# Token differences and the third LayerNorm's normalisation on GpSimd, in a fused attention and channel-mixing kernel

## The chip, the cores and the metric

The kernel runs as one program on the 8 cores of one Trainium2 chip. Each core computes one half (2048 tokens) of one of four sequences, with 512 tokens ahead of it for the attention window. The metric is the device time in microseconds of the slowest core.

## The reference, cut to what matters

```python
x = x + _layernorm(_L0_attn_ref(_layernorm(x), w_qkv, w_out))      # 16 heads of 64, window 512, RoPE
x = x + _layernorm(_L0_ffn_ref(_layernorm(x), W_r, W_k, W_v, mu_r, mu_k))
...
# in _L0_ffn_ref
x_prev = jnp.concatenate([jnp.zeros((B, 1, C), x.dtype), x[:, :-1, :]], axis=1)
xr = mu_r * x + (1.0 - mu_r) * x_prev
xk = mu_k * x + (1.0 - mu_k) * x_prev
r = jax.nn.sigmoid(jnp.einsum('btc,dc->btd', xr, W_r))
k = jnp.einsum('btc,dc->btd', xk, W_k)
k_act = jnp.square(jax.nn.relu(k))
out = r * jnp.einsum('btc,dc->btd', k_act, W_v)
```

The model width is 1024. The kernel computes the two mixtures as `x_prev + mu * (x - x_prev)`, so each needs the token difference `x - x_prev` once.

## The kernel before, in words

Each core works through 20 tiles of 128 tokens. Tiles 0 to 2 give keys and values only; tiles 3 to 19 are also queries. The order of the work is written out by hand: `slot_table` places every step (`"k0"`, `"norm1"`, `"mix"`, ...) in a numbered slot, and each engine runs one program that loops over the slots and issues what it has in each, after waiting on semaphores. Slots are not times. An engine that has nothing to wait for runs ahead, and one that waits holds all that it has in later slots.

**Attention part.** A tile takes 16 slots, one per head. Per head TensorE makes scores (L583), VectorE adds the mask and takes the maximum (`row_max`, L764), ScalarE takes the exponential (`exps`, L935), a DMA transposes it, and TensorE weights the values (L604). Between the heads lie the next tile's projections (L520), the rotary embedding (VectorE L742 and L745, then an addition on GpSimd, L1096), the output projection (L674), and the second LayerNorm with its residual addition on GpSimd (L1106), which gives x2, the input of the second half. x2 is stored to a spill tensor in HBM.

**Second half.** Its 16 tiles are taken in four groups of four (`sup` 0 to 3); one more tile, i = 0, gives the token ahead. Per tile: `stats3` (VectorE statistics, L774 to L777), `rstd3` (ScalarE, L917 and L919), `norm3` (VectorE L787, `(x - mean) * rstd` from f32 to bf16), `tx` (TensorE transposes, L690), and `x2T_out` (ScalarE, into `x2T`, L950). When a group's tiles are in `x2T`, `mix_chunk` makes the inputs of its products in 8 chunks of 512 tokens, all on VectorE: the difference into `dch`, which is `xl2a` (L813), a drain, xk (L815) and xr (L817), the last two `scalar_tensor_tensor` with both tensor inputs in SBUF. From the second group on the first chunk also copies the last token of the group before (L805). The last chunk lets TensorE start on the group.

A group's products are 24 units of 8 matmuls each, one per slot, in the order of `UNITS`: eight `fk` (L703), then `fr` (L715) and `fv` (L730) mixed. ScalarE makes relu and square of `fk` (L956, L960) and the sigmoid of `fr` in three steps (L971, L973, L975). VectorE multiplies the sigmoid with `fv` and takes statistics (`ff_out`, L832 to L838); ScalarE applies the fourth LayerNorm (L1066), and GpSimd adds the residual (`ob`, L1124). Unit n of group `sup` is in slot `F_OFF + 24 sup + n`. The chunks of the next group's mixing lie in that group's slots 14 to 21, and its `tx` in slots 4, 6, 8 and 10. The first four tiles of `sup` 0 and tile i = 0 are handled early, during attention (`EARLY_SLOT`), and the mixing of `sup` 0 lies in slots 315 to 322, among the heads of the last attention tile.

Of the kernel before, what the change touches and what calls it, by code (L numbers as in the profile page):

```python
# [74 lines left out]
F_OFF = 329  # L75
# [15 lines left out]
CAST0 = 79  # L91
# [142 lines left out]
def build_nc():  # L234
# [27 lines left out]
    with es:  # L262
# [10 lines left out]
        with ExitStack() as p1:  # L273
# [505 lines left out]
            def norm3(ve, i):  # L779
# [5 lines left out]
                elif i >= 5:  # L785
                    ve.wait_ge(S["mm"], mm_no("qt", NT - 1))
# [457 lines left out]
```

## Time and profile before

| what | value |
|---|---|
| runs shown | median 730.37 us, 729.66 to 730.95, 3 runs |
| profiled execution | 729.59 us; span of the slowest core 728.1 us |
| spans of the eight cores | 723.4 to 728.1 us |
| busy in the span | TensorE 616.1, VectorE 560.3, ScalarE 537.6, GpSimd 207.5 us |
| granted TensorE clock, mean of the core shown | 0.965 |

The span runs from the first to the last instruction of the slowest core, and 1.5 us of the profiled time lie around it. Busy time is the time in which an engine executes something; where it waits for another engine the trace names the one that released it. Times in the rows are counted from the span's start.

### The profile page before, as it was taken

What the parts mean: (1) busy time and instruction counts of PE and PEld (TensorE: products, weight loads), DVE (VectorE), ACT (ScalarE), POOL (GpSimd) and SP (SyncE); (2) the same over time, 40 slices, a digit from 0 to 9 for tenths busy, and PEclk for the clock granted to TensorE, in tenths of its full rate; (3) what the DMA queues carried; (4) which work ended last, traced back from release to release, by engine and by line L of the source; (5) the groups of instructions that cost most, each with busy time, mean ns of one, the idle gap of its engine ahead of it and who ended that gap; (6) DMA issues with size and microseconds to landing.
All of it is one profiled execution on the core that took longest, in us unless ns stands there. A gap on an engine that the chain in (4) does not pass through costs nothing.

```text
span 728.1 us, 15852 instructions; the slowest of 8 cores (723.4 to 728.1 us)
## 1 busy us (share of the span) xinstructions
PE 616.1 (85%) x4680; PEld 326.2 (45%) x4680; DVE 560.3 (77%) x1143; ACT 537.6 (74%) x1060; POOL 207.5 (28%) x184
## 2 busy tenths in 40 slices
PE   1978799989989999989899999955997896896993
PEld 0434445545555545555555555523543442442441
DVE  3563788998998988989888988899559759759234
ACT  2135779888988988998888898856884784693773
POOL 3561032143143144134134313401013403303213
PEclk9999999999999999999999999985999999999998
DMA  7999889978998999989998876898824244313304
GB/s 171 180 185 156 146 152 178 174 148 163 168 152 153 164 156 183 172 157 181 154 164 162 151 159 133 157 249 190 234 94 187 67 145 145 112 63 116 116 1 173
DMA packets 202738, 111.21 MB, mean 153 GB/s; under 512 B 181408, under 2 KB 184736, under 8 KB 202272
## 3 DMA queue, kind: packets, MB, share of 16 engines
q1 hardware_dynamic: 197536, 95.52, 61.7%
q0 software_dynamic: 5120, 14.68, 13.5%
q8 instruction: 40, 0.66, 0.4%
q14 instruction: 42, 0.34, 0.2%
HBM read 62.99 MB, written 23.59 MB: 119 GB/s over the span
## 4 chain that ended last, share of the span: by engine, by line
PE 50%; DVE 18%; DVEq 10%; issue 10%; ACT 5%; POOL 2%; DMA 2%; ACTq 1%; SPq 0%; POOLq 0%
PE PS L520 19%; PE PS L583 6%; PE PS L674 6%; PE PS L715 5%; PE PS L703 4%; DVEq L834 4%; PE PS L604 3%; DVE sneg L764 3%; PE PS L513 3%; PE PS L533 3%; DVE tmpAB L745 2%; DVE tmpAB L742 2%; DVEq L814 2%; ACT Pn L935 2%; POOL kqnat L1096 2%
## 5 line engine op out<-in xcount | busy, mean ns | idle before, releaser
L764 DVE CUSTOM_DVE_ANT_0 sneg<-PS,mqs 128x640 f32<-128x640 f32 (+1 forms) x272 | 215.8, 813 | 51.5 <-PE PS L583 43.5
L935 ACT ACTIVATE Pn<-sneg,nm 128x640 bf16<-128x640 f32 (+1 forms) x272 | 221.2, 814 | 37.7 <-DVE nm L764 36.1
L520 PE MATMUL PS<-wbig,xll 128*128 128x512 bf16 x768 | 181.0, 379 | 6.4 <-DVE tmpAB L745 4.1
L583 PE MATMUL PS<-kT,qEO 128*128 128x128 bf16 (+3 forms) x656 | 113.5, 279 | 23.1 <-DVE nm L764 22.9
L1096 POOL TENSOR_TENSOR kqnat<-tmpAB 128x512 bf16<-128x512 f32 x74 | 94.4, 1278 | 114.0 <-DVE tmpAB L745 114.0
L520 PEld LDWEIGHTS PS<-wbig,xll 128*128 128x128 bf16 x768 | 69.4, 97 | 82.9 <-issue 11.8
L583 PEld LDWEIGHTS PS<-kT,qEO 128*128 128x128 bf16 x656 | 53.9, 98 | 65.6 <-issue 36.1
L1101 POOL TENSOR_SCALAR st<-st 128x1 f32<-128x1 f32 x17 | 4.5, 266 | 246.2 <-ACT st L919 246.2
L674 PE MATMUL PS<-wout_b,oTs 128*128 128x512 bf16 x272 | 64.2, 378 | 1.6 <-DVE sneg L832 1.0
L604 PE MATMUL PS<-v_nat,PT 128*128 128x64 bf16 x1344 | 62.4, 194 | 3.6 <-DMA PT<-Pn 2.5
L917 ACT ACTIVATE st<-st,sb_consts 128x1 f32<-128x1 f32 x70 | 20.4, 291 | 56.4 <-DVE st L890 22.8
L742 DVE TENSOR_TENSOR tmpAB<-PS,sb_tabs 128x512 f32<-128x512 f32 x74 | 50.8, 687 | 13.4 <-PE PS L533 9.3
L604 PEld LDWEIGHTS PS<-v_nat,PT 128*128 128x128 bf16 x1344 | 53.2, 99 | 16.1 <-issue 5.3
L730 PE MATMUL PS<-wbig,xll 128*128 128x512 bf16 x256 | 57.4, 379 | 0.0
L832 DVE TENSOR_TENSOR sneg<-PS,qEO 128x512 f32<-128x512 f32 x32 | 21.9, 684 | 44.2 <-PE PS L730 42.2
L935 ACT ACTIVATION_READ_ACCUMULATOR Pn<-sneg,nm 128x1 f32 x272 | 51.7, 190 | 0.0
L745 DVE TENSOR_TENSOR tmpAB<-PS,sb_tabs 128x512 f32<-128x512 f32 x74 | 50.4, 680 | 0.0
L1106 POOL TENSOR_TENSOR xb<-xb,t 128x1024 f32<-128x1024 f32 x17 | 40.3, 2370 | 12.2 <-ACT t L1048 12.2
L703 PE MATMUL PS<-Pn,wbig 128*128 128x512 bf16 x128 | 31.8, 412 | 10.7 <-DVE PT L817 10.7
L730 PEld LDWEIGHTS PS<-wbig,xll 128*128 128x128 bf16 x256 | 25.0, 98 | 30.3 <-issue 0.6
L513 PE MATMUL PS<-sb_ident,kqnat 128*128 128x128 bf16 x296 | 22.9, 221 | 18.2 <-POOL kqnat L1096 16.2
L674 PEld LDWEIGHTS PS<-wout_b,oTs 128*128 128x128 bf16 x272 | 24.3, 97 | 30.1 <-issue 4.6
(92 smaller groups left out, 932.6 us busy)
## 6 DMA issues: line engine op xcount, KB each, us to landing
xb<-x_ext SPq DMA_DIRECT2D x20, 512.0 KB, 4.9
x2spill<-xb SPq DMA_DIRECT2D x17, 512.0 KB, 3.0
wbig<-wqkv POOLq DMA_DIRECT2D x12, 512.0 KB, 21.4
wbig<-wff SPq DMA_DIRECT2D x12, 512.0 KB, 5.2
kT<-x2spill SPq DMA_DIRECT2D x9, 512.0 KB, 5.5
out<-kT SPq DMA_DIRECT2D x9, 512.0 KB, 3.0
tmpAB<-x2spill SPq DMA_DIRECT2D x8, 512.0 KB, 5.6
v_nat<-x2spill SPq DMA_DIRECT2D x7, 512.0 KB, 5.5
```

Source lines behind the costliest of these rows:

```text
L513: last = pe.transpose(PSb[:, col + c * 128:col + (c + 1) * 128], src[:, base + c * 128:base + (c + 1) * 128], ident[:])
L520: last = pe.matmul(PSf[:, col:col + 512], xlt_part(t, c * 128, 128), wslice(base, c, lo, 512), start=(c == 0), stop=(c == 7))
L583: last = pe.matmul(PSf[:, col:col + nb * 128], qq[:, qc:qc + 128], kT[:, kc:kc + nb * 128], start=True, stop=True)
L604: last = pe.matmul(PSf[:, col:col + 64], PT[:, pc:pc + 128], v_nat[:, vc:vc + 64], start=(kb == first_kb), stop=(kb == 4))
L674: last = pe.matmul(PSf[:, col:col + 512], oTs[:, c * 128:(c + 1) * 128], wout_b[:, c * 1024 + h * 512:c * 1024 + h * 512 + 512], start=(c ...
L703: last = pe.matmul(PSf[:, col:col + 512], wslice(1, c, j * 128, 128), xk_half[sup % 2][:, c * 512:c * 512 + 512], start=(c == 0), stop=(c ...
L730: last = pe.matmul(PSf[:, col:col + 512], kaT[:, c * 512 + o * 128:c * 512 + o * 128 + 128], wslice(2, c, h * 512, 512), start=(c == 0), s ...
L742: ve.tensor_tensor(bass.AP(tmpAB, toff, [[2048, 128], [64, 8], [32, 2], [1, 32]]), bass.AP(PS, base, [[4096, 128], [64, 8], [32, 2], [1, 3 ...
L745: ve.tensor_tensor(bass.AP(tmpAB, 1024 + toff, [[2048, 128], [64, 8], [32, 2], [1, 32]]), bass.AP(PS, base + 32, [[4096, 128], [64, 8], [- ...
L764: ve.tensor_tensor_reduce(out=sneg[:, dst + lo:dst + 640], in0=PSf[:, col + lo:col + 640], in1=mqs[:, mcol + lo:mcol + 640], scale=-0.125, ...
L935: sc.activation(Pn[:, dst + lo:dst + 640], sneg[:, src + lo:src + 640], AF.Exp, bias=nm[:, hc:hc + 1], scale=-1.0, accum_out=rs[:, hc:hc + ...
L1096: gp.tensor_tensor(dst[:, (i % 2) * 512:(i % 2) * 512 + 512], tmpA[:, toff:toff + 512], tmpB[:, toff:toff + 512], ALU.add).then_inc(S["nat ...
```

## The change

GpSimd takes two things from VectorE. `norm3` moves to the GpSimd program, for all 17 tiles. The difference becomes a step of its own, `"dif"`, on GpSimd: `difference` writes it to the place where xr will stand (`xr_half`), and VectorE's chunk then makes xk from it and xr in place, after a wait on the new semaphore `dif`. The drain between the difference and the two others is gone, and the copy of the last token moves along. For `sup` 0 the eight differences are spread over slots 192 to 297, for the others they stand four slots ahead of their chunks. Other slots are set anew: the second half starts one slot earlier (`F_OFF` 329 to 328), `norm3` two slots earlier in its group, `ob`, `store` and `res` one or two later, the loads of the `fr` weights two later, and the slots of the first tiles and the bank rotation's end (`HEAD_END`) change. Branches for tiles 90 and up never apply, as there are 20 tiles.

```diff
-    3: {"xload": -22, "tabload": -22, "stats1": -8, "rstd1": -5, "norm1": 1, "x": 3,
-        "k0": 31, "k1": 32, "kt": 40, "qt": 44, "v0": 67, "v1": 68},
+    3: {"xload": -23, "tabload": -22, "stats1": -6, "rstd1": -5, "norm1": 2, "x": 5,
+        "k0": 31, "k1": 33, "kt": 40, "qt": 42, "v0": 67, "v1": 68},
...
-KG = 28
-QG = 37
-V0_SLOT = {"0": 59, "1": 60, "2": 62, "3": 64}
+KG = 26
+QG = 35
+V0_SLOT = {"0": 59, "1": 60, "2": 61, "3": 62}
...
-F_OFF = 329
+F_OFF = 328
...
-EARLY_SLOT = {"stats3": 54, "rstd3": 56, "norm3": 58, "tx": 60}
-MASK_OFF = 0
+EARLY_SLOT = {"stats3": 54, "rstd3": 56, "norm3": 59, "tx": 60}
+MASK_OFF = -1
...
-ITEM_SLOT = {"ld": -6, "stats3": -1, "rstd3": -1, "norm3": 1, "tx": 3}
+ITEM_SLOT = {"ld": -6, "stats3": -1, "rstd3": -1, "norm3": -1, "tx": 3}
...
-OUT_LAG = {"ff": 2, "rstd4": 2, "nb4": 2, "t2": 3, "ob": 3, "store": 7, "res": 0}
-WF_SLOT = {"wfk": 303, "wfr": 310, "wfv": 321}
+
+DIF0 = 192
+DIF_STEP = 15
+DIF_LEAD = 4
+OUT_LAG = {"ff": 2, "rstd4": 2, "nb4": 2, "t2": 3, "ob": 4, "store": 9, "res": 1}
+WF_SLOT = {"wfk": 303, "wfr": 312, "wfv": 321}
...
-HEAD_END = 59
+HEAD_END = 49
...
+            table[("dif", F_OFF + 24 * sup - MIX_LEAD + c - DIF_LEAD)] = 8 * sup + c
+        table[("dif", DIF0 + DIF_STEP * c)] = c
...
-                d = dch[:, (c % 2) * 512:(c % 2) * 512 + 512]
-                x = bass.AP(x2T, cur + c * 520 + 8, [[8320, 128], [1, 512]])
-                xp = bass.AP(x2T, cur + c * 520 + 7, [[8320, 128], [1, 512]])
-                ve.tensor_tensor(d, x, xp, ALU.subtract)
-                ve.drain()
-                ve.scalar_tensor_tensor(xk_half[sup % 2][:, c * 512:(c + 1) * 512], d, mus[:, 8 + c:9 + c], xp,
-                                        ALU.mult, ALU.add)
-                last = ve.scalar_tensor_tensor(xr_half[sup % 2][:, c * 512:(c + 1) * 512], d, mus[:, c:c + 1], xp,
-                                               ALU.mult, ALU.add)
+                d = xr_half[sup % 2][:, c * 512:(c + 1) * 512]
+                xp = bass.AP(x2T, cur + c * 520 + 7, [[8320, 128], [1, 512]])
+                ve.wait_ge(S["dif"], u + 1)
+                ve.scalar_tensor_tensor(xk_half[sup % 2][:, c * 512:(c + 1) * 512], d, mus[:, 8 + c:9 + c], xp,
+                                        ALU.mult, ALU.add)
+                last = ve.scalar_tensor_tensor(d, d, mus[:, c:c + 1], xp, ALU.mult, ALU.add)
...
+            def difference(gp, u):
+
+                sup, c = divmod(u, 8)
+                cur = (sup % 2) * 4160
+                if c == 0:
+                    gp.wait_ge(empty_sem("tx", 4 + 4 * sup), empty_cnt("tx", 4 + 4 * sup))
+                    if sup == 1:
+                        gp.wait_ge(S["av"], NQ * 8)
                     if sup >= 1:
                         prv = ((sup - 1) % 2) * 4160
-                        ve.tensor_copy(bass.AP(x2T, cur + 7, [[8320, 128], [520, 8], [1, 1]]),
+                        gp.tensor_copy(bass.AP(x2T, cur + 7, [[8320, 128], [520, 8], [1, 1]]),
                                        bass.AP(x2T, prv + 519, [[8320, 128], [520, 8], [1, 1]]))
-                        ve.drain()
+                        gp.drain()
                     if sup >= 2:
-                        ve.wait_ge(S["mm"], mm_no("fr", (sup - 2) * 8 + 7))
+                        gp.wait_ge(S["mm"], mm_no("fr", (sup - 2) * 8 + 7))
+                gp.tensor_tensor(xr_half[sup % 2][:, c * 512:(c + 1) * 512],
+                                 bass.AP(x2T, cur + c * 520 + 8, [[8320, 128], [1, 512]]),
+                                 bass.AP(x2T, cur + c * 520 + 7, [[8320, 128], [1, 512]]),
+                                 ALU.subtract).then_inc(S["dif"], 1)
...
+                if i >= 2:
+                    ve.wait_ge(S["xl2"], i - 1)
...
+            def norm3(gp, i):
+                gp.wait_ge(S["rstd3"], i + 1)
+                if 1 <= i < 5:
+                    gp.wait_ge(S["mm"], mm_no("tx", i - 1))
+                elif i >= 7:
+                    gp.wait_ge(S["mm"], mm_no("tx", i - 2))
+                elif i >= 5:
+                    gp.wait_ge(S["mm"], mm_no("qt", NT - 1))
+                gp.tensor_scalar(xl2_part(i, 0, 1024), x2_tile(i), stat2(st3, i, 12, 1),
+                                 stat2(st3, i, 14, 1), ALU.subtract, ALU.mult).then_inc(S["xl2"], 1)
```

## Rows read from the trace of the kernel before

**Rows 1.** The page: the span and the busy times of the engines.

```profile
span 728.1 us, 15852 instructions; the slowest of 8 cores (723.4 to 728.1 us)
...
PE 616.1 (85%) x4680; PEld 326.2 (45%) x4680; DVE 560.3 (77%) x1143; ACT 537.6 (74%) x1060; POOL 207.5 (28%) x184
```

**Rows 2.** Waits of the whole span: who waited for whom, us in total, times, longest.

```profile
PE PS L583 <- DVE nm L764: 22.9, 25, 3.3
...
PE PS L703 <- DVE PT L817: 10.7, 2, 6.6
...
PE PS L703 <- DVE xr L817: 6.9, 1, 6.9
...
PE PS L690 <- DVE kqnat L787: 4.2, 4, 1.9
```

**Rows 3.** Windows: busy time of each engine by stretch, clock, DMA share, GB/s.

```profile
102.00:204.00 102.00, 93.23 (x861) 53.05 (x856) 92.96 (x208) 90.24 (x188) 30.59 (x30) 1.00 0.91 162
...
480.00:500.00 20.00, 6.88 (x66) 4.13 (x63) 19.34 (x36) 8.29 (x18) 2.86 (x2) 0.64 0.95 222
...
506.40:564.60 58.20, 53.19 (x334) 26.06 (x332) 40.99 (x68) 41.27 (x77) 8.45 (x6) 1.00 0.57 183
564.60:619.40 54.80, 45.16 (x224) 20.69 (x224) 40.93 (x64) 37.15 (x67) 14.16 (x10) 0.94 0.35 120
619.40:672.70 53.30, 45.15 (x225) 20.68 (x226) 39.80 (x62) 35.41 (x64) 11.38 (x8) 0.95 0.26 90
672.70:716.30 43.60, 43.60 (x192) 19.09 (x192) 14.32 (x25) 30.81 (x54) 10.13 (x8) 0.95 0.26 92
```

**Rows 4.** Timeline of VectorE, the mixing among the last heads: start, us, what.

```profile
475.91 0.42 DVE L813 TENSOR_TENSOR xl2a<-x2T 128x512 bf16<-128x512 bf16 x1
...
477.75 0.82 DVE L764 CUSTOM_DVE_ANT_0 sneg<-PS,mqs 128x640 f32<-128x640 f32 x1
...
500.06 0.81 DVE L764 CUSTOM_DVE_ANT_0 sneg<-PS,mqs 128x640 f32<-128x640 f32 x1
```

**Rows 5.** Timeline of TensorE: the start of groups 1, 2 and 3, idle time in brackets.

```profile
564.59 8.53 PE L703 MATMUL PS<-Pn,wbig 128*128 128x512 bf16 x32 [4.06 <-DVE PT L817]
...
619.43 8.42 PE L703 MATMUL PS<-xb,wbig 128*128 128x512 bf16 x32 [6.91 <-DVE xr L817]
...
672.66 16.01 PE L703 MATMUL PS<-Pn,wbig 128*128 128x512 bf16 x64 [6.64 <-DVE PT L817]
```

**Rows 6.** Groups of instructions by line and shape: busy us, mean ns of one.

```profile
L1096 POOL TENSOR_TENSOR kqnat<-tmpAB 128x512 bf16<-128x512 f32 x74 | 94.4, 1278 | 114.0 <-DVE tmpAB L745 114.0
...
L835 DVE BATCH_NORM_STATS2 st<-sneg 128x6 f32<-128x512 f32 x32 | 22.2, 694 | 3.3 <-issue 0.4
L832 DVE TENSOR_TENSOR sneg<-PS,qEO 128x512 f32<-128x512 f32 x32 | 21.9, 684 | 44.2 <-PE PS L730 42.2 <-POOL kT L1124 1.9
L1124 POOL TENSOR_TENSOR kT<-kT,sneg 128x1024 f32<-128x1024 f32 x9 | 21.1, 2348 | 18.1 <-ACT sneg L1066 18.1
...
L815 DVE SCALAR_TENSOR_TENSOR xb<-xl2a,sb_mus,x2T 128x512 bf16<-128x512 bf16 x16 | 15.9, 992 | 1.2
L813 DVE TENSOR_TENSOR xl2a<-x2T 128x512 bf16<-128x512 bf16 x32 | 14.9, 464 | 0.4
...
L1116 POOL TENSOR_SCALAR st<-st 128x1 f32<-128x1 f32 x15 | 6.6, 440 | 101.0 <-ACT st L919 101.0
...
L787 DVE TENSOR_SCALAR xl2a<-xb,st 128x1024 bf16<-128x1024 f32 x5 | 4.0, 808 | 0.0
```

**Rows 7.** Timeline of all engines in group 1: GpSimd beside VectorE's two-input instructions.

```profile
593.88 1.01 ACT L950 ACTIVATE x2T<-PS 128x1024 bf16<-128x1024 bf16 x1
...
601.75 0.39 POOL L1116 TENSOR_SCALAR st<-st 128x1 f32<-128x1 f32 x1 [18.61 <-ACT st L919]
...
603.69 2.37 POOL L1124 TENSOR_TENSOR v_nat<-v_nat,sneg 128x1024 f32<-128x1024 f32 x1 [1.54 <-ACT sneg L1066]
603.77 2.84 DVE L817 SCALAR_TENSOR_TENSOR xr<-xl2a,sb_mus,x2T 128x512 bf16<-128x512 bf16 x1
...
613.23 0.77 POOL L1116 TENSOR_SCALAR st<-st 128x1 f32<-128x1 f32 x1 [7.17 <-ACT st L919]
```

More of the change, by code:

```diff
@@ L86 @@
 MIX_LEAD = 10
-OUT_LAG = {"ff": 2, "rstd4": 2, "nb4": 2, "t2": 3, "ob": 3, "store": 7, "res": 0}
-WF_SLOT = {"wfk": 303, "wfr": 310, "wfv": 321}
+DIF0 = 192
[3 more added lines that the diff above has]
+WF_SLOT = {"wfk": 303, "wfr": 312, "wfv": 321}
 WF_STEP = 6
-CAST0 = 79
+CAST0 = 78
 CAST_STEP = 8
@@ L777, in stats3 @@
                 ve.bn_aggr(stat2(st3, i, 12, 2), stat2(st3, i, 0, 12)).then_inc(S["mv3"], 1)
-            def norm3(ve, i):
-                ve.wait_ge(S["rstd3"], i + 1)
-                if 1 <= i < 5:
-                    ve.wait_ge(S["mm"], mm_no("tx", i - 1))
-                elif i >= 7:
-                    ve.wait_ge(S["mm"], mm_no("tx", i - 2))
-                elif i >= 5:
-                    ve.wait_ge(S["mm"], mm_no("qt", NT - 1))
-                ve.tensor_scalar(xl2_part(i, 0, 1024), x2_tile(i), stat2(st3, i, 12, 1),
-                                 stat2(st3, i, 14, 1), ALU.subtract, ALU.mult).then_inc(S["xl2"], 1)
             def mix_chunk(ve, u):
@@ L802, in mix_chunk @@
                             ve.wait_ge(ptsem(pr), 16 * (pr // PR + 1))
+                    if sup >= 2:
+                        ve.wait_ge(S["mm"], mm_no("fr", (sup - 2) * 8 + 7))
+                d = xr_half[sup % 2][:, c * 512:(c + 1) * 512]
[3 more added lines that the diff above has]
+                                        ALU.mult, ALU.add)
@@ L803, in mix_chunk @@
+                last = ve.scalar_tensor_tensor(d, d, mus[:, c:c + 1], xp, ALU.mult, ALU.add)
+                if c == 7:
+                    last.then_inc(S["mix"], 1)
+            def difference(gp, u):
[5 more added lines that the diff above has]
+                        gp.wait_ge(S["av"], NQ * 8)
                     if sup >= 1:
@@ L819, in mix_chunk @@
-                if c == 7:
-                    last.then_inc(S["mix"], 1)
+                        gp.wait_ge(S["mm"], mm_no("fr", (sup - 2) * 8 + 7))
[3 more added lines that the diff above has]
+                                 ALU.subtract).then_inc(S["dif"], 1)
             def ff_out(ve, u):
@@ L868, in vector_program @@
                     if t is not None:
+                        if t >= 92:
+                            ve.wait_ge(S["xln"], t - 1)
                         ve.wait_ge(xsem(t), 16 * (t // XR + 1))
@@ L874, in vector_program @@
                     t = tile_at(n, "norm1")
-                    if t is not None:
+                    if t is not None and t < 90:
                         ve.wait_ge(S["rstd1"], t + 1)
@@ L890, in vector_program @@
                         ve.bn_aggr(stat(st2, t, 12, 2), stat(st2, t, 0, 12)).then_inc(S["mv2"], 1)
-                    i = tile_at(n, "norm3")
-                    if i is not None:
-                        norm3(ve, i)
                     i = tile_at(n, "stats3")
@@ L1102, in gpsimd_program @@
                                          ALU.mult, ALU.mult).then_inc(S["nb2"], 1)
+                    t = tile_at(n, "norm1")
+                    if t is not None and t >= 90:
+                        gp.wait_ge(S["rstd1"], t + 1)
+                        gp.wait_ge(S["mm"], mm_no("x", t - 2))
+                        gp.tensor_scalar(xln[:, (t % 2) * 1024:(t % 2) * 1024 + 1024], x_tile(t), stat(st1, t, 12, 1),
+                                         stat(st1, t, 14, 1), ALU.subtract, ALU.mult).then_inc(S["xln"], 1)
+                    i = tile_at(n, "norm3")
+                    if i is not None:
+                        norm3(gp, i)
+                    u = tile_at(n, "dif")
+                    if u is not None:
+                        difference(gp, u)
                     t = tile_at(n, "add2")
```

7 lines of the change are left out of this document (3 added, 4 removed), and 12 rows, old and new, of tables (HEAD_SLOT, SEMS).

## The prediction

> **What bounds the kernel now.** I read the page first, for the busy times: TensorE leads with 616.1 of 728.1 us, VectorE follows with 560.3, and GpSimd has the room, 28% [rows 1]. An average says little here, so I cut the span into stretches [rows 3]. The reader is to see three regimes. In the attention part (one stretch of 102 us shown) TensorE has 93.2, VectorE 93.0 and ScalarE 90.2 us of 102: three engines hold each other, none is alone the bound. From 480 to 500 us VectorE has 19.3 us of 20 and TensorE 6.9: there VectorE alone is the bound, and the granted clock falls to 0.64. In the second half groups 0, 1 and 2 take 58.2, 54.8 and 53.3 us, while group 3, which has no mixing behind it, takes 43.6 with TensorE busy throughout. So what groups 1 and 2 have over about 43.5 us is waiting.
>
> The waits say for whom [rows 2]: TensorE waited 22.9 us for `row_max`, most of it between 478 and 504 us, 17.6 us for the last xr of a mixing (three times), and 4.2 us for norm3. The timelines place them. The mixing of group 0 runs from 475.91 to 500.06, eight chunks with seven heads' maxima and the one at 500.06 behind them [rows 4]. At the start of groups 1, 2 and 3 TensorE stood idle for 4.06, 6.91 and 6.64 us, and then ran its first four units in 8.5 us where later ones take 6.9 (at 1.2 instead of 2.4 GHz for some of it) [rows 5].
>
> **What the change takes from VectorE.** The difference takes 0.42 us, and with the drain a chunk goes from 1.84 us (475.91 to 477.75) to the two remaining instructions, 1.84 - 0.50 = 1.34 us [rows 4]. The mean of 464 ns over 32 holds a few that were held up [rows 6]. norm3 takes 0.81 us of VectorE per tile where nothing holds it [rows 6].
>
> **What it adds to GpSimd.** No row shows a bf16 difference or a wide `tensor_scalar` on GpSimd. The floor is the one-column instruction of L1116, mean 0.44 us; the ceiling is the two-input addition of 1024 f32, 2.35 us; the nearest row is the two-input addition of 512 elements with bf16 output, 1.28 us, and I take that for the difference [rows 6]. For norm3 (1024 elements, one tensor input) I take 1.3 us, between the same ends. Nothing hangs on it: in the second half norm3 stands ready four slots before its transposes, and GpSimd is busy for 14.2 of 54.8 us in group 1 [rows 3]. With the new work that becomes about 14.2 + 8 x 1.28 + 4 x 1.3 = 29.6 us. If that cover were gone, TensorE's 4.2 us of waits for norm3 would stay. The new wait in `stats3` only keeps a statistics slot from being overwritten two tiles on; behind it in VectorE's queue stands `ff_out`, and norm3 two tiles back is long done.
>
> **The cost that is not in the instruction times.** VectorE's two remaining mixing instructions read two SBUF tensors, and so does GpSimd's difference. The trace shows what happens when such a pair meets. At 603.69 GpSimd starts its residual addition and needs its usual 2.37 us; the xr instruction at 603.77 takes 2.84 us instead of 0.75, and ends 0.55 us after GpSimd does [rows 7]. That is waiting, not sharing. It works the other way too: L1116 takes 0.39 us at 601.75 and 0.77 at 613.23, each time ending just behind a two-input VectorE instruction [rows 7]. The mean of 992 ns on L815 [rows 6] against 0.75 unheld is such collisions. The Trainium skill has a rule for it (SBUF — State Buffer, Who interferes with whom): a VectorE instruction with two SBUF inputs and a GpSimd instruction that reads SBUF exclude each other, the second waiting for the whole of the first. The trace agrees, with 2.84 against 0.75 us. By that rule the moved differences are not parallel to the mixing at all; without it each mixing would lose the full 4.0 us worked out below.
>
> **The sum, in the order of time.**
>
> Head (0 to 80 us): the order of TensorE's products there is nearly the same, and the first 20 us wait for loads. I take 0, with 1.5 us to either side.
>
> Attention: five norm3 leave VectorE, 5 x 0.73 us of queue time = 3.7 us. ScalarE and TensorE are as full as VectorE [rows 3], so I count a quarter: -0.9. The eight differences of group 0, 10 us in all, lie in slots that hold no rotary addition on GpSimd, and VectorE's heads read PSUM there; bounds 0 and -3.7.
>
> Mixing of group 0: here VectorE is the bound, and no difference runs beside it since all eight were made long before. 8 x 0.50 = 4.0 us come off in full: -4.0. The second half starts one slot earlier, in a stretch in which TensorE idles anyway: a head's spacing, about 1.6 us: -1.6.
>
> Mixings of groups 1, 2 and 3. I follow the one beside group 1. Its first `ff_out` starts at 593.8, and the last xr ends at 619.1, where TensorE had been free since 612.5 (619.43 - 6.91) [rows 5]. GpSimd's first difference must wait for `x2T_out` of the group's last tile, which ends at 593.88 + 1.01 = 594.9 [rows 7]. From then on 8 differences x 1.28 = 10.2 us and 16 instructions x 0.67 = 10.7 us exclude each other, so the end can't come before 594.9 + 20.9 = 615.8. If VectorE keeps its pairs together and its `ff_out` (0.68 + 0.69 us, one SBUF input or none [rows 6]) falls beside differences, I get 616.2: -2.9. If GpSimd gets in between every two VectorE instructions while it has differences queued, and its residual addition (2.35 us) gets in too, the differences run ahead and the mixing ends at about 620.5: +1.4. The 601.75 row (in between xk and xr) speaks for the second, the 613.23 row (past one more instruction) for the first. I take the middle, -0.8, for the mixings beside groups 1 and 2. For the one beside group 0 the same two countings give 561 and 564.8 against 564.1 before, because there the first difference can start two slots ahead of the first chunk: -1.2. Sum of the three: -2.8.
>
> Group 3 and the tail hold no mixing and no norm3: 0. `ob`, `store` and `res` later by a slot or two are waited for by nothing until the very end, where each is driven by its data.
>
> Total: -0.9 - 4.0 - 1.6 - 2.8 = -9.3 us against the execution's own 729.59, so 720.3. The median of the runs shown is 0.8 above that execution: 721.
>
> **The rivals.** What can be told from no change is about 0.2%, 1.5 us.
>
> *Forecast* (716 to 727), chance 0.48.
>
> *The exclusion costs little and TensorE becomes the bound* (chance 0.22). GpSimd's differences might slip into VectorE's `ff_out` times, or cost well under 1.28 us with bf16 inputs. Then the idle times before groups 1 to 3 and the waits for norm3 go, 17.6 + 4.2 = 21.8 us. Taking 70% of it, since ScalarE with 37.2 of 54.8 us [rows 3] runs some 5 us behind by `x2T_out`: 729.6 - 5.6 - 0.9 - 15.3 = 707.8, or 708 to 709 beside the median, 700 to 715 as ends. For it: the room on GpSimd. Against it: 594.9 as the first possible start.
>
> *Full alternation* (chance 0.18): each of the three mixings ends 1 to 1.5 us later than before, and only group 0's gain remains: 729.6 - 5.6 + 3.5 + 0.8 = 728, 727 to 731. Half of it counts as no change.
>
> *The difference is dear* (chance 0.12), the side on which it is slower. If the bf16 difference costs 2.35 us like the widest row [rows 6], each of the 24 differences of the later mixings adds 1.07 us to the excluded time: 24 x 1.07 = 25.7, so 720.3 + 25.7 = 746. It decides from 1.28 + 9.3/24 = 1.67 us on. For it: no row shows bf16 inputs on GpSimd, one of them at an odd element. Against it: 1.28 and 2.35 us are in proportion to the elements, not to bytes, since one writes bf16 and the other f32. The Trainium skill (GPSIMD Engine Reference, Engine selection) says that elementwise work belongs on VectorE, GpSimd being about twice slower with two inputs. The trace has 1.28 against 0.42 us, three times, and the rule is about the engine, not about which of them is waited for.
>
> **How the numbers follow.** Faster by over 0.2%: 0.48 + 0.22 + 0.08 = 0.78; within: 0.10; slower: 0.12. The range leaves out the dear difference, the deepest part of the TensorE case and the upper end of the alternation: 706 to 730; the forecast's own is 716 to 727.
>
> **What would show it.** L815 and L817 mean times above 1 us in the later mixings and near 0.75 in group 0's; the GpSimd difference near 1.28 us; 24 of the differences beside or between VectorE's pairs; the mixing of group 0 in about 20 us instead of 24; TensorE still idle for 3 to 8 us before groups 1 to 3; groups 1 and 2 at 52 to 56 us. Wrong it would be if those groups fall below 49 us, if the bf16 difference is far from 1.28 us, or if the attention part changes by more than 4 us.

## The result and the profile after

The changed kernel takes 734.27 us (median of 11 runs) beside 730.95 us of the kernel before (11 runs). The ratio is 1.0049, with a 95% interval of 1.0032 to 1.0066: slower by about 0.5%, or 3.6 us. Three of the 11 runs of before (754, 774 and 781 us) were in a slower state of the chip, and such runs are left out of all ratios here and of the means over runs, not of the medians. The forecast was 721 us, with a range of 706 to 730. It had the wrong sign.

The page of after, with its busy times, stands beside [rows 1]. The profiled execution took 738.41 us, which is the highest of the 11 runs, and the core shown is its slowest.

```profile
span 736.9 us, 15874 instructions; the slowest of 8 cores (724.8 to 736.9 us)
...
PE 624.0 (85%) x4680; PEld 327.4 (44%) x4680; DVE 536.4 (73%) x1091; ACT 538.9 (73%) x1060; POOL 311.8 (42%) x236
```

VectorE lost 24 us of work and GpSimd gained 104 us. By the forecast's prices, 32 differences of 1.28 us and 17 `norm3` of 1.3 us, GpSimd would have gained 63 us.

Because single cores lie up to 12 us apart, I compare stages by their mean over the eight cores of the profiled execution. The marks are the first row maximum (L764 before, L769 after: the end of the head) and the first `fk` product (L703, L708: the start of the second half). These are one execution of each kernel. Over all its runs the mean span of a kernel spreads by 0.2 to 1.0 us (standard deviation), and the execution shown of the changed kernel lies 1.5 us above the mean of its 11 runs (729.9 against 728.4), so differences below about 1 us say little.

| mean of 8 cores, us | head | attention to first fk | second half | span |
|---|---|---|---|---|
| before | 62.2 | 441.6 | 221.8 | 725.6 |
| after | 66.2 | 438.3 | 225.4 | 729.9 |
| difference | +4.0 | -3.3 | +3.6 | +4.3 |
| forecast | 0 | -6.5 | -2.8 | -9.3 |

The middle stage went the right way. The head and the second half went the wrong way, by 4.0 and 6.4 us against the forecast. The waits of the whole span say for whom in the second half; they answer to [rows 2].

```profile
PE PS L588 <- DVE nm L769: 28.0, 37, 2.9
...
PE PS L695 <- POOL kqnat L1089: 13.5, 7, 2.4
DVE st L781 <- POOL kqnat L1089: 10.5, 5, 4.8
...
PE PS L735 <- DVE sneg L840: 5.8, 4, 2.5
...
PE PS L538 <- DMA wbig<-wqkv: 5.2, 2, 3.7
...
PE PS L708 <- DVE PT L806: 3.2, 1, 3.2
...
PE PS L708 <- DVE xr L806: 2.6, 1, 2.6
```

TensorE's wait for the last xr before a group of products went from 17.6 us in three times to 5.8 in two, a larger fall than the forecast's. In its place stand 13.5 us in which it waits for `norm3` (L1089, now on GpSimd), where it was 4.2 us, and 7.1 us (5.8 at L735 and 1.3 at L708) in which it waits for `ff_out` (L840) to empty the PSUM bank that the next product needs, where it was 1.0. VectorE itself waits 10.5 us for `norm3` inside `stats3`. Another 5.2 us are waits of the query products (L538) for their weights' loads. The windows of after, beside [rows 3], show whose engine filled up (102 to 204 us of attention, 20 us around group 0's mixing, then groups 0, 1, 2 and 3):

```profile
102.00:204.00 102.00, 93.51 (x844) 52.53 (x845) 91.83 (x208) 89.78 (x185) 41.40 (x33) 1.00 0.99 156
...
484.00:504.00 20.00, 8.31 (x86) 5.19 (x84) 19.78 (x36) 10.77 (x24) 2.87 (x2) 0.72 1.08 219
...
509.30:567.90 58.60, 54.02 (x337) 26.25 (x335) 35.77 (x54) 41.28 (x77) 32.97 (x18) 0.99 0.57 170
567.90:624.50 56.60, 45.93 (x226) 20.80 (x226) 33.61 (x52) 37.77 (x68) 39.95 (x24) 0.97 0.37 121
624.50:681.50 57.00, 45.84 (x224) 20.71 (x224) 33.89 (x49) 35.76 (x64) 37.30 (x21) 0.96 0.28 84
681.50:725.30 43.80, 43.76 (x190) 19.21 (x191) 14.40 (x25) 30.86 (x54) 11.65 (x9) 0.93 0.27 97
```

In group 1 GpSimd is busy for 39.95 of 56.6 us, where the forecast had 29.6. Groups 1 and 2 take 56.6 and 57.0 us, not 52 to 56. Group 3, which holds no mixing and no norm3, takes 43.8 us, where it took 43.6. The prices are in the groups by form:

```profile
L1089 POOL TENSOR_SCALAR kqnat<-tmpAB,st 128x1024 bf16<-128x1024 f32 x8 | 30.2, 3778 | 12.5 <-PE PS L708 11.4 <-ACT st L926 1.2
...
L825 POOL TENSOR_TENSOR PT<-x2T 128x512 bf16<-128x512 bf16 x16 | 21.1, 1343 | 3.7 <-issue 3.7
...
L806 DVE SCALAR_TENSOR_TENSOR PT<-PT,sb_mus,x2T 128x512 bf16<-128x512 bf16 x16 | 19.5, 1216 | 0.0
...
L804 DVE SCALAR_TENSOR_TENSOR Pn<-PT,sb_mus,x2T 128x512 bf16<-128x512 bf16 x16 | 17.1, 1069 | 4.1 <-POOL PT L825 4.1
```

The difference (L825) costs 1.34 us in the mean, collisions with VectorE included, close to the 1.28 taken. `norm3` costs 3.78 us against 0.81 on VectorE [rows 6], where 1.3 was taken. The timeline of GpSimd in the first half of group 1 shows what that makes:

```profile
574.67 3.77 POOL L1089 TENSOR_SCALAR kqnat<-tmpAB,st 128x1024 bf16<-128x1024 f32 x1 [0.42 <-ACT st L926]
578.42 0.26 POOL L1146 TENSOR_SCALAR st<-st 128x1 f32<-128x1 f32 x1
578.65 2.36 POOL L1154 TENSOR_TENSOR kT<-kT,sneg 128x1024 f32<-128x1024 f32 x1
580.99 3.78 POOL L1089 TENSOR_SCALAR kqnat<-xb,st 128x1024 bf16<-128x1024 f32 x1
584.73 2.35 POOL L1154 TENSOR_TENSOR v_nat<-v_nat,sneg 128x1024 f32<-128x1024 f32 x1
587.07 3.77 POOL L1089 TENSOR_SCALAR kqnat<-tmpAB,st 128x1024 bf16<-128x1024 f32 x1
590.80 2.34 POOL L1136 TENSOR_TENSOR xb<-xb,t 128x1024 f32<-128x1024 f32 x1
593.13 3.78 POOL L1089 TENSOR_SCALAR kqnat<-tmpAB,st 128x1024 bf16<-128x1024 f32 x1
```

Look at the brackets: after the first line there are none, so GpSimd works without a pause from 574.67 to 596.9 us. Four `norm3` alternate with three residual additions, and each waits in the queue for the one ahead. TensorE's transposes stand right behind three of them, and stop the products of the group:

```profile
578.59 0.61 PE L695 MATMUL PS<-sb_ident,kqnat 128*128 128x128 bf16 x8 [2.16 <-POOL kqnat L1089]
...
584.91 0.85 PE L695 MATMUL PS<-sb_ident,kqnat 128*128 128x128 bf16 x8 [2.26 <-POOL kqnat L1089]
...
597.05 0.61 PE L695 MATMUL PS<-sb_ident,kqnat 128*128 128x128 bf16 x8 [2.01 <-POOL kqnat L1089]
```

### The profile page after: what moved, and what is told of

Its sections match the earlier page's. It is cut to its first block, busy times and chain, and to the rows that moved or that the text cites. A ratio compares the mean times of both kernels' runs of the same rounds, so it can differ in the third digit from the quotient of the medians.

```text
span 736.9 us, 15874 instructions; the slowest of 8 cores (724.8 to 736.9 us)
## 1 busy us (share of the span) xinstructions
PE 624.0 (85%) x4680; PEld 327.4 (44%) x4680; DVE 536.4 (73%) x1091; ACT 538.9 (73%) x1060; POOL 311.8 (42%) x236
## 4 chain that ended last, share of the span: by engine, by line
PE 44%; DVE 15%; issue 10%; DMA 10%; POOL 7%; ACT 5%; DVEq 5%; ACTq 2%; SPq 1%; POOLq 0%
PE PS L525 18%; PE PS L588 5%; DMA PT<-Pn 5%; PE PS L708 5%; PE PS L679 4%; PE PS L720 4%; DMA wbig<-wqkv 4%; POOL kqnat L1089 3%; DVEq L842 3%; PE PS L609 3%; DVE sneg L769 3%; PE PS L518 2%; ACT Pn L942 2%; DVE tmpAB L747 2%; PE PS L735 2%
## 5 line engine op out<-in xcount | busy, mean ns | idle before, releaser
L769 DVE CUSTOM_DVE_ANT_0 sneg<-PS,mqs 128x640 f32<-128x640 f32 (+1 forms) x272 | 216.4, 814 | 57.2 <-PE PS L588 53.3
L525 PE MATMUL PS<-wbig,xll 128*128 128x512 bf16 x768 | 184.8, 385 | 5.9 <-DVE tmpAB L750 4.5
L840 DVE TENSOR_TENSOR sneg<-PS,qEO 128x512 f32<-128x512 f32 x32 | 21.8, 683 | 63.5 <-PE PS L735 61.1
L609 PE MATMUL PS<-v_nat,PT 128*128 128x64 bf16 x1344 | 62.4, 194 | 5.4 <-DMA PT<-Pn 5.4
L735 PE MATMUL PS<-wbig,xll 128*128 128x512 bf16 x256 | 58.0, 379 | 5.8 <-DVE sneg L840 5.8
L924 ACT ACTIVATE st<-st,sb_consts 128x1 f32<-128x1 f32 x70 | 20.3, 290 | 40.1 <-DVE st L883 14.4
L978 ACT ACTIVATE qEO<-PS 128x512 f32<-128x512 f32 x32 | 18.9, 592 | 31.4 <-DVE sneg L840 17.6
L735 PEld LDWEIGHTS PS<-wbig,xll 128*128 128x128 bf16 x256 | 24.6, 98 | 36.5 <-issue 7.7
L679 PEld LDWEIGHTS PS<-wout_b,oTs 128*128 128x128 bf16 x272 | 24.4, 97 | 29.6 <-issue 4.0
L708 PE MATMUL PS<-Pn,wbig 128*128 128x512 bf16 x128 | 32.9, 420 | 4.5 <-DVE PT L806 3.2
```

The source lines that it names most:

```text
L525: last = pe.matmul(PSf[:, col:col + 512], xlt_part(t, c * 128, 128), wslice(base, c, lo, 512), start=(c == 0), stop=(c == 7))
L609: last = pe.matmul(PSf[:, col:col + 64], PT[:, pc:pc + 128], v_nat[:, vc:vc + 64], start=(kb == first_kb), stop=(kb == 4))
L679: last = pe.matmul(PSf[:, col:col + 512], oTs[:, c * 128:(c + 1) * 128], wout_b[:, c * 1024 + h * 512:c * 1024 + h * 512 + 512], start=(c ...
L708: last = pe.matmul(PSf[:, col:col + 512], wslice(1, c, j * 128, 128), xk_half[sup % 2][:, c * 512:c * 512 + 512], start=(c == 0), stop=(c ...
L735: last = pe.matmul(PSf[:, col:col + 512], kaT[:, c * 512 + o * 128:c * 512 + o * 128 + 128], wslice(2, c, h * 512, 512), start=(c == 0), s ...
L769: ve.tensor_tensor_reduce(out=sneg[:, dst + lo:dst + 640], in0=PSf[:, col + lo:col + 640], in1=mqs[:, mcol + lo:mcol + 640], scale=-0.125, ...
```

## The experiments

The times are medians; each ratio is to the kernel before, run on the same chip, with its 95% interval. The stage lengths are again means over eight cores of one execution.

### 1. norm3 back on VectorE

The changed kernel, with `norm3` in VectorE's program and at its old slots, and without the wait in `stats3`. The differences stay on GpSimd.

```diff
-EARLY_SLOT = {"stats3": 54, "rstd3": 56, "norm3": 59, "tx": 60}
+EARLY_SLOT = {"stats3": 54, "rstd3": 56, "norm3": 58, "tx": 60}
...
-ITEM_SLOT = {"ld": -6, "stats3": -1, "rstd3": -1, "norm3": -1, "tx": 3}
+ITEM_SLOT = {"ld": -6, "stats3": -1, "rstd3": -1, "norm3": 1, "tx": 3}
...
+                        norm3(ve, i)
...
-                        norm3(gp, i)
```

> The changed kernel with norm3 back on VectorE in its old slots; the differences stay on GpSimd. Theory 1 (norm3's price on GpSimd, 3.78 us a tile in the changed kernel's trace against 0.81 on VectorE, holds TensorE's transposes in groups 1 and 2): the four waits of TensorE for norm3 (2.2, 2.3, 0.3, 2.0 us) shrink to 1 or 2 us in all per group, and the second half, from the first fk to the end of the span, falls from a mean of 225.5 us over the cores to 218 to 220; the kernel comes out 5 to 7 us faster than the changed one, near 728. Theory 2 (the differences and VectorE's two-input instructions excluding each other is what costs): the second half stays at 224 to 226 us and the kernel at 733 to 735. In both, the first row maximum stays at 64 to 68 us.

Measured: 726.63 us, ratio 0.9936 (0.9912 to 0.9959). The head stays at 66.4, the second half falls from 225.4 to 218.5 us, the mean span from 729.9 to 721.5. By these two executions `norm3` on GpSimd costs 8.4 us, 6.9 of them in the second half; by the mean spans over all runs it is 6.7 (728.4 against 721.7). The edit takes out the price and the new wait in `stats3` together, so what that wait costs by itself isn't shown.

### 2. The head's slots of before

The changed kernel with the slots of the first tiles (`HEAD_SLOT`), `KG`, `QG`, `V0_SLOT` and `HEAD_END` as before.

```diff
...
-KG = 26
-QG = 35
-V0_SLOT = {"0": 59, "1": 60, "2": 61, "3": 62}
+KG = 28
+QG = 37
+V0_SLOT = {"0": 59, "1": 60, "2": 62, "3": 64}
...
-HEAD_END = 49
+HEAD_END = 59
```

> The changed kernel with the slots of the first tiles of before (HEAD_SLOT, KG, QG, V0_SLOT, HEAD_END); all else as changed. Theory 3 (the new slots of the first tiles cost time, since TensorE waits for the query weights ahead of work that could go first): the first row maximum comes at 61 to 64 us instead of 64.5 to 68.5, and the kernel is 3 to 4 us faster than the changed one, near 730.5. Rival (the later start of the heads is made up for in the attention part, or is chance of the loads): the first row maximum stays at 64 to 68, or moves and the time stays within 1 us of the changed kernel's, 733 to 735.

Measured: 728.98 us, 0.9974 (0.9954 to 0.9995). The head is back at 62.4 us and the second half is as in the changed kernel, 224.7.

### 3. Both

> Both edits together: norm3 on VectorE and the slots of the first tiles of before. If theories 1 and 3 both hold their gains add: 734.3 - 6 - 3.5 = 724 to 725, faster than before by 0.8%. If only the exclusion of differences and mixing matters, 733 to 735; if only the head, 730 to 731.

Measured: 722.62 us, 0.9881 (0.9857 to 0.9904). Head 61.8, attention 436.6, second half 218.2, mean span 716.6 us. That is 9.0 us below before's 725.6, and 8.6 by the means over all runs (717.5 against 726.1). What remains of the change is the differences on GpSimd, the slots of the second half and the mask's load one slot earlier. For that the forecast had 8.4 us, its 9.3 without the 0.9 of `norm3`.

### 4. norm3 on GpSimd alone

The kernel before, with only `norm3` moved (the reverse of the edit of experiment 1). All differences stay on VectorE.

> The kernel before with norm3 alone moved to GpSimd, in the slots of the changed kernel (the statistics wait for norm3 two tiles back as there). Theory 1: norm3 takes about 3.8 us there too, the residual additions between them delay it, TensorE waits 6 to 8 us per group in groups 1 and 2 for its transposes, and as VectorE's mixing runs late in any case some of it adds: 734 to 738. Theory 2: it relieves VectorE and costs nothing: 727 to 730.

Measured: 742.87 us, 1.0156 (1.013 to 1.0183), dearer than expected. The attention stage stays at 441.0, the second half takes 233.4 instead of 221.8 us, and group 1 alone goes from 54.8 to 62.7 us (core shown). The move costs 11.5 us of mean span where nothing else is changed, and 8.4 (after against experiment 1) or 7.6 (experiment 2 against 3) with the differences moved as well. By the means over all runs these are 10.8, 6.7 and 6.5. Why it is dearer alone wasn't tried. The trace says only that 13.9 us of waits for `norm3` stand there beside 16.5 for the last xr and 0.6 for `ff_out`, where the changed kernel has 13.5, 5.8 and 7.1.

### 5. One slot of the head

Experiment 3's kernel with `QG = 35`, all else of the head as before.

```diff
-QG = 37
+QG = 35
```

> The kernel of both edits (norm3 on VectorE, first tiles' slots of before) with one slot number of the changed kernel put back: QG 35, so that TensorE's products for tile 3's queries stand ahead of the key transposes of tile 2 instead of behind them. Theory 3 in its narrow form: the products wait for the query weights' loads, the transposes and the rotary additions on GpSimd wait behind them, and the first row maximum comes 3 to 5 us later, at 65 to 67 us: 726 to 727. Rival (other slots of the first tiles are the cause: KG, V0_SLOT, HEAD_END): the first row maximum stays at 60 to 63 us and the time within 1 us of the 722.6.

Measured: 725.45 us, 0.9922 (0.9904 to 0.994). The head goes from 61.8 to 65.6 us. The other way round, the changed kernel with `QG = 37` alone:

> The changed kernel with the one slot number of the queries' first products put back to that of before: QG 37. If this slot alone is what the new first slots cost, the first row maximum comes at 61 to 64 us and the kernel is as fast as with all the first slots of before (728.98), 728 to 730.5. Rival (it takes several of them): the first row maximum at 64 us or later, 732 to 734.

Measured: 729.6 us, 0.9989 (0.9969 to 1.0008), head 62.5 against 66.2 us. With one number set back, the changed kernel can't be told from the kernel before. The timeline of TensorE in the head of the changed kernel, on the core shown, has the mechanism:

```profile
36.75 1.89 PE L538 MATMUL PS<-wbig,oTs 128*128 128x512 bf16 x8
...
40.19 1.02 PE L538 MATMUL PS<-wbig,oTs 128*128 128x512 bf16 x4 [1.55 <-DMA wbig<-wqkv]
...
44.90 1.87 PE L538 MATMUL PS<-wbig,oTs 128*128 128x512 bf16 x4 [3.69 <-DMA wbig<-wqkv]
46.56 1.06 PE L518 MATMUL PS<-sb_ident,kqnat 128*128 128x128 bf16 x8
```

The first query products now stand ahead of tile 2's key transposes (L518). Their weights have not landed, TensorE waits 1.55 and 3.69 us for the loads, and the transposes wait behind them in its queue. GpSimd, which makes the next keys by the rotary addition into the buffer that those transposes read, then waits too, in its own timeline:

```profile
47.77 2.49 POOL L1114 TENSOR_TENSOR kqnat<-tmpAB 128x512 bf16<-128x512 f32 x2 [8.68 <-PE PS L518]
```

In the kernel before the transposes (L513) went first, and the query products ran without a wait behind them:

```profile
41.26 0.61 PE L513 MATMUL PS<-sb_ident,kqnat 128*128 128x128 bf16 x8 [2.33 <-POOL kqnat L1096]
41.77 5.30 PE L533 MATMUL PS<-wbig,oTs 128*128 128x512 bf16 x16
```

### 6. What the later differences are worth

Experiment 3's kernel with the differences of groups 1 to 3 made on VectorE again, as in the kernel before. Group 0's stay on GpSimd.

```diff
-                ve.wait_ge(S["dif"], u + 1)
+                if sup == 0:
+                    ve.wait_ge(S["dif"], u + 1)
+                else:
...
+                    ve.tensor_tensor(d, bass.AP(x2T, cur + c * 520 + 8, [[8320, 128], [1, 512]]), xp, ALU.subtract)
+                    ve.drain()
```

> The kernel of both edits with the differences of groups 1 to 3 made on VectorE again, as before (with their drain and the token copy); those of group 0 stay on GpSimd. By the terms of the prediction (three later mixings, -2.8 us together) this is 2 to 4 us slower than the 722.6, and the second half rises from 218.2 to about 221. Rival A (GpSimd's differences take from VectorE as much as they save): within 1 us, 722 to 723.5, second half 218 to 219. Rival B (they are worth their full 4.0 us per mixing): 729 or more, second half at 225 or more.

Measured: 722.81 us, 0.9888 (0.9859 to 0.9917), which experiment 3's 0.9881 can't be told from. The second half takes 219.3 against 218.2 us. So 24 of the 32 differences bring at most 1 us, nothing that the times of the kernel can show, and 2.5 of the 3.6 us by which experiment 3's second half is shorter than before's are there without them. What this kernel keeps from the change are the slots of the second half (`ob`, `store`, `res`, the weights' loads, `F_OFF`), group 0's differences on GpSimd, and the place to which a difference is written. Which of them brings the 2.5 us wasn't tried.

### 7. The last transpose's exit first

If VectorE's and GpSimd's instructions exclude each other, the mixing's end is set by the start of the first difference, which waits for `x2T_out` on ScalarE. In its program `x2T_out` stands behind the `kact_out` and `sig_out` of the same slot. This is experiment 3's kernel with it ahead of them:

```diff
+                    i = tile_at(n, "tx")
+                    if i is not None:
+                        x2T_out(sc, i)
                     u = tile_at(n, "fk")
...
-                    i = tile_at(n, "tx")
-                    if i is not None:
-                        x2T_out(sc, i)
```

> The kernel of both edits with one step moved on ScalarE: in each slot it empties the second half's transposes into x2T (x2T_out) ahead of the relu or sigmoid of the same slot's product, as TensorE makes them in that order. If the start of the differences, which wait for the group's last x2T_out, sets when the mixing ends, the first difference starts about 2 us earlier and groups 1 and 2 get 1 to 2 us shorter each: 719 to 721. Rival (the time in which GpSimd and VectorE exclude each other, or TensorE, sets it): within 1 us of 722.6.

Measured: 712.38 us, 0.9739 (0.9719 to 0.9759), much more than expected, and the fastest kernel of the study. Second half 208.1 us; group periods 58.8, 48.9 and 48.0 us against 59.8, 54.0 and 51.2 in experiment 3. The starts of groups 1 and 2 on TensorE and the first difference of group 1's mixing in experiment 3:

```profile
560.50 1.67 PE L708 MATMUL PS<-Pn,wbig 128*128 128x512 bf16 x7
...
606.71 1.89 PE L735 MATMUL PS<-wbig,xll 128*128 128x512 bf16 x8 [1.95 <-DVE sneg L849]
609.41 1.89 PE L735 MATMUL PS<-wbig,xll 128*128 128x512 bf16 x8 [0.81 <-DVE sneg L849]
614.54 8.75 PE L708 MATMUL PS<-xb,wbig 128*128 128x512 bf16 x32 [3.25 <-DVE xr L815]
```

```profile
591.30 0.22 POOL L829 COPY x2T<-x2T 128x8 bf16<-128x8 bf16 x1 [12.96 <-ACT x2T L969]
```

and the same in experiment 7, with `x2T_out` itself:

```profile
561.62 3.62 PE L708 MATMUL PS<-Pn,wbig 128*128 128x512 bf16 x16
...
610.56 7.07 PE L708 MATMUL PS<-xb,wbig 128*128 128x512 bf16 x32 [2.83 <-DVE xr L815]
```

```profile
587.52 1.01 ACT L969 ACTIVATE x2T<-PS 128x1024 bf16<-128x1024 bf16 x1
...
588.66 0.22 POOL L829 COPY x2T<-x2T 128x8 bf16<-128x8 bf16 x1 [10.81 <-ACT x2T L969]
```

Counted from the group's start, the first difference comes at 27.0 us instead of 30.8, and from there to the next group's start it takes 21.9 us instead of 23.2. Of the 3.8 us, 2.1 lie between the group's last transposes and the first difference, on ScalarE (5.7 instead of 7.9 us); the other 1.6 come from the transposes themselves, which TensorE reaches sooner. The first four units of the next group then take 7.07 us at a granted clock of 1.00 (all of it at 2.4 GHz), instead of 8.75 us at 0.81 (some of it at 1.2 GHz). TensorE's wait at the border hardly changes (2.83 instead of 3.25 us). What goes are its stops inside the group: in experiment 3 it waits 1.95 and 0.81 us for `ff_out` (L849) to empty a PSUM bank, while VectorE is held up in the chunks, and in experiment 7 for neither.

The same edit on the kernel before, where the difference is VectorE's:

> The kernel before, without any of the change, with ScalarE's x2T_out moved ahead of the relu or sigmoid of the same slot. If what that step gained (10 us, 722.6 to 712.4) is the earlier start of GpSimd's differences, it gains nothing or under 2 us here, where the mixing on VectorE waited for nothing from it: 729 to 731, second half 220 to 222. Rival (it frees PSUM banks or transposes for TensorE, or shortens ScalarE's queue, whoever makes the differences): 4 to 10 us faster, 721 to 727, second half at 212 to 218.

Measured: 730.48 us, 1.0001 (0.9981 to 1.0022). No gain. And experiment 7's kernel with the later differences on VectorE (last row of the table below):

> As the fastest kernel so far (both edits, x2T_out first), with the differences of groups 1 to 3 on VectorE. If the move of these differences pays only once x2T_out comes early, this is 4 us or more slower than 712.4: 716 to 722. If it pays nothing in either order, as it did in the other one (722.8 against 722.6), 711.5 to 714.

Measured: 722.74 us, 0.989 (0.9861 to 0.9919). Counted from experiment 6, which has neither edit (0.9888), the later differences on GpSimd alone give nothing that can be measured (0.9881), nor does the early exit alone (0.989), and both together give 10 us (0.9739). TensorE's waits in the second half, summed and averaged over the eight cores, show where the gain of each edit stays:

| TensorE waits, us | for the last xr | for `ff_out` | second half |
|---|---|---|---|
| before | 17.4 | 1.1 | 221.8 |
| experiment 3 (differences on GpSimd, late exit) | 6.0 | 9.7 | 218.2 |
| experiment 6 (later ones on VectorE, late exit) | 16.3 | 0.7 | 219.3 |
| experiment 7 (on GpSimd, early exit) | 5.6 | 3.2 | 208.1 |
| experiment 7 with later ones on VectorE | 16.2 | 1.2 | 219.4 |

With the late `x2T_out`, moving the differences takes 10 us of waits for the last xr away and puts 9 us of waits for `ff_out` in their place. With the early one the first part stays gone and only 2.0 us come back (3.2 against 1.2). While VectorE makes the differences, the early exit changes neither wait.

### 8. The mixing one slot earlier

Experiment 7's kernel with the chunks one slot ahead, the differences at the same slots.

```diff
-MIX_LEAD = 10
-DIF_LEAD = 4
+MIX_LEAD = 11
+DIF_LEAD = 3
```

> As the fastest kernel so far, with VectorE's chunks of the mixing one slot earlier in groups 1 to 3 (MIX_LEAD 11, DIF_LEAD 3; GpSimd's differences stay in their slots). TensorE still waits 2.8 us for the last xr before groups 2 and 3. If the mixing's end is set by VectorE's queue, it ends up to 1.7 us earlier per group and the kernel is 1 to 4 us faster: 708 to 711. If the exclusion with GpSimd sets it, or the held-up ff_out costs as much, 711 to 715.

Measured: 715.98 us, 0.9803 (0.9774 to 0.9832), slower than experiment 7 by 3.6 us. TensorE's idle time before groups 2 and 3 falls to 0.32 and 1.41 us, but the groups take 60.1, 49.5 and 49.8 us. The wait at the border moved into the group, and grew there. Averaged over the cores TensorE waits 2.4 us for the last xr where it was 5.6, and 9.5 us for `ff_out` where it was 3.2: the chunks one slot earlier stand ahead of an `ff_out` that has to empty a bank. One of their instructions meets GpSimd's residual addition and takes 2.46 us, `ff_out` starts at 606.87 behind it, and TensorE, which waits 2.54 us for it, goes on at 607.69:

```profile
603.82 2.46 DVE L813 SCALAR_TENSOR_TENSOR xb<-xr,sb_mus,x2T 128x512 bf16<-128x512 bf16 x1
```

### 9. What an operation costs on GpSimd

For prices only. Experiment 3's kernel, with the `norm3` of the early tiles on GpSimd in another form for each; it leaves out part of the third LayerNorm for these tiles.

```diff
...
+                if i == 0 or i == 3:
+                    last = gp.tensor_scalar(xl2_part(i, 0, n), x2_tile(i)[:, 0:n], mean, rstd, ALU.subtract, ALU.mult)
+                elif i == 1:
+                    last = gp.tensor_scalar(xl2_part(i, 0, n), x2_tile(i), mean, None, ALU.subtract)
+                elif i == 2:
+                    last = gp.tensor_scalar(xl2_part(i, 0, n), x2_tile(i), 0.0, 1.0, ALU.subtract, ALU.mult)
+                else:
+                    last = gp.tensor_copy(xl2_part(i, 0, n), x2_tile(i))
```

> The kernel of both edits with norm3 of the five early tiles on GpSimd in different forms, to price them: tile 0 the full form on 1024 columns (two operations, mean and rstd read per partition), tile 1 the subtraction of the mean alone, tile 2 two operations with constants in place of mean and rstd, tile 3 the full form on 512 columns, tile 4 a plain copy to bf16. It leaves out part of the third LayerNorm for these tiles. If the price is per element and operation, tile 1 takes about half of 3.78 us and tile 3 about 1.9; if reading the two statistics per partition is what costs, tile 2 takes under 1.5 us; if the write to bf16 costs, all 1024-column forms lie near 3.8 us, the copy too.

Measured, in the timeline of GpSimd (both operations; subtraction only; both with constants; both on 512 columns; a copy):

```profile
131.79 3.77 POOL L1102 TENSOR_SCALAR xl2a<-xb,st 128x1024 bf16<-128x1024 f32 x1 [0.81 <-ACT st L940]
...
158.67 2.85 POOL L1104 TENSOR_SCALAR xl2a<-xb,st 128x1024 bf16<-128x1024 f32 x1 [0.86 <-ACT st L940]
...
185.51 3.64 POOL L1106 TENSOR_SCALAR xl2a<-xb 128x1024 bf16<-128x1024 f32 x1 [0.85 <-ACT st L940]
...
212.38 2.07 POOL L1102 TENSOR_SCALAR xl2a<-xb,st 128x512 bf16<-128x512 f32 x1 [0.87 <-ACT st L940]
...
239.20 1.03 POOL L1108 CAST xl2a<-xb 128x1024 bf16<-128x1024 f32 x1 [0.83 <-ACT st L940]
```

The scalars read from memory and the write to bf16 cost next to nothing (3.77 against 3.64; the copy writes bf16 too). The two operations do: a copy takes 1.03 us, one operation 2.85, two 3.77. Each form but the full one stands on a single instruction. From 512 to 1024 columns are 1.70 us, 3.3 ns a column, over a fixed 0.37 us (2.07 - 1.70), if the time is a straight line between these two sizes. The whole kernel took 727.08 us in this one run.

## Why the prediction was wrong, step by step

**The step that failed: the price of `norm3`, and the sentence "Nothing hangs on it".** The term was 1.3 us, between ends of 0.44 and 2.35 us. It is 3.77, outside both ends. The ceiling was the dearest instruction that the trace showed, a two-input addition; taking it for a ceiling assumed that one tensor input is never dearer than two. The cover was an occupancy, 29.6 of 54.8 us, and an average doesn't hide anything: the four `norm3` of a group lie in slots 0 to 6, and with three residual additions make 4 x 3.78 + 3 x 2.35 = 22.2 us of GpSimd in a row. The slots where TensorE wants the results, 4 to 10, fall into the same stretch, and the transposes stand in the same queue as the group's products. The forecast even said what it would cost if the cover were gone, "TensorE's 4.2 us of waits for norm3 would stay"; they grew to 13.5 us. Experiments 1 and 4 show the price from both sides: over all runs 6.7 us taken away and 10.8 us added (8.4 and 11.5 in the executions shown). The forecast's gain of 0.9 us in the attention part, from `norm3` leaving VectorE, didn't come either: that stage took 438.3, 437.1 and 437.5 us in the three kernels with both moves (after, experiment 2, and `QG = 37` alone in experiment 5), and 436.6 and 436.7 with `norm3` back on VectorE (experiments 3 and 1). The new wait in `stats3`, by the forecast for something "long done", held VectorE for 10.5 us. With `norm3` back, the second half is 3.3 us shorter than before (218.5), where the forecast had 2.8.

**The second step that failed: the head, "0, with 1.5 us to either side".** The argument was that the order of TensorE's products is nearly the same. Nearly was the trouble: one slot number puts the query products ahead of a tile's key transposes, and at that point the query weights are still on their way. The two runs of experiment 5 give 3.8 and 3.7 us of head for that number. The diff showed `QG = 35`, and the slot table and the trace of before would have shown which product passes which wait.

**The third step that failed: the path in the later mixings.** The forecast followed only the end of the last xr and priced `ff_out` by its own time. It left out that TensorE needs `ff_out` to empty its banks. In experiment 3 the wait for the last xr falls by 11.4 us, and 8.6 of them come back as waits for `ff_out`. In its number it cost the forecast under 2 us (-2.8 where the moved differences brought some -1.1), but it hid the 10 us that experiment 7 found.

**What was right.** Up to the first `fk`, mixing of group 0 and slot together were to give 5.6 us, and in experiment 3, where `norm3` is on VectorE, the stage gained 5.0 (441.6 to 436.6). No run has group 0's part alone, but the trace of the changed kernel shows it:

```profile
483.33 0.75 DVE L804 SCALAR_TENSOR_TENSOR xb<-xr,sb_mus,x2T 128x512 bf16<-128x512 bf16 x1
...
503.67 0.81 DVE L769 CUSTOM_DVE_ANT_0 sneg<-PS,mqs 128x640 f32<-128x640 f32 x1
```

From the first chunk to the maximum behind the last it takes 20.3 us, where [rows 4] have 24.15: 3.8 of the 4.0 us. The difference was taken at 1.28 us: in the attention part the eight took 1.03 to 1.06, and the mean of the 16 that write `PT` is 1.34. So the dear difference, from 1.67 us on, is excluded. The exclusion held too: the chunk's instructions took 1.07 and 1.22 us in the mean (L804 and L806 of groups 1 and 3) instead of 0.75, and beside a queued difference about 1.5. The first chunk in experiment 3, in the timeline of GpSimd and VectorE:

```profile
591.73 7.37 POOL L834 TENSOR_TENSOR xr<-x2T 128x512 bf16<-128x512 bf16 x6 [0.21 <-issue]
...
592.88 1.44 DVE L813 SCALAR_TENSOR_TENSOR xb<-xr,sb_mus,x2T 128x512 bf16<-128x512 bf16 x1 [1.93 <-POOL xr L834]
...
594.24 1.52 DVE L815 SCALAR_TENSOR_TENSOR xr<-xr,sb_mus,x2T 128x512 bf16<-128x512 bf16 x1
```

Both are doubled: GpSimd's next difference gets in between two VectorE instructions that stand ready one behind the other. That is the alternation of the second countings, the one that the 601.75 row spoke for. The Trainium skill (SBUF — State Buffer, Who interferes with whom) calls the port pair that the two engines share an exclusive lock, and says that the order of issue decides who is blocked. The trace agrees, with 1.44 and 1.52 us where 0.75 is the unheld time. From the first difference to the next group's start are 614.54 - 591.30 = 23.2 us; the forecast's two countings made it 21.3 and 25.6, so the middle that it took was right there.

**Right in sum, not in its parts.** With both costs undone the kernel gains 9.0 us, or 8.6 over all runs (experiment 3), against the 8.4 left of the forecast. That is partly luck. Of the -2.8 us for the later mixings the moved differences are some 1.1 (219.3 to 218.2), which the times can't tell from none (experiment 6), and another 2.5 come with what else that kernel keeps of the change, which the forecast took at nothing. And the rival in which TensorE becomes the bound, 708 us, was closer to what the idea can give than the forecast was: with one exit moved it is 712.38, though TensorE still waits there for VectorE (8.8 us in the table of experiment 7). The forecast had named the obstacle, "594.9 as the first possible start", and took it as given, not as a place in ScalarE's program that an edit can move.

**A rule that warned in one half and misled in the other.** The Trainium skill (GPSIMD Engine Reference, Engine selection) has elementwise work on VectorE and calls GpSimd about twice as slow for two inputs and roughly at line rate for one. The trace agrees for two inputs (the moved difference, 1.04 against 0.42 us, 2.5 times) and nearly for a copy with one input, 1.03 us for 1024 columns (a VectorE copy wasn't measured; its `tensor_scalar` takes 0.81), and not for the `tensor_scalar` with one input and two operations, 3.77 us against VectorE's 0.81. The measurement decides: 4.7 times as slow. The forecast weighed the rule for the difference alone, where it was not the dear part; for `norm3` its second half would have spoken for a price near VectorE's.

## What to carry to other kernels

An operation that the trace doesn't show on the engine it moves to has no ceiling there, and the dearest neighbour isn't one: work out from which price on it decides, and for which instructions it stands in a row without a gap, before saying that nothing hangs on it. Cover is a matter of the slots next to the waiter, not of the engine's share of the span. When work taken off a full engine gains nothing, look at which wait has taken the place of the old one, and at what the moved work's input waits for in the third engine's program: here two edits, each worth nothing alone, were worth 10 us together.

## What the runs showed of the hardware

A `tensor_scalar` on GpSimd from f32 to bf16, 128x1024: 3.77 us with two operations, 2.85 with one, 1.03 for a copy; with two operations 0.37 us + 3.3 ns a column, from two sizes. On VectorE the same instruction takes 0.81 us. The two-input addition of 1024 f32 takes GpSimd 2.35 us, so there one input with two operations is dearer than two inputs with one.

GpSimd's queued differences get in between two consecutive two-input VectorE instructions, which then take 1.44 and 1.52 us instead of 0.75, and the six differences take 7.37 us, 1.23 each instead of 1.04.
